# Moving the first half's expert choice and part of its scatters into the attention turns

## The reference

```python
x = x + tanh(g_xattn[0]) * attention(layernorm(x), ctx, ctx, mask, Wq, bq, Wk, bk, Wv, bv, Wo, bo)   # 16 heads of 8
x = x + tanh(g_ffn[0]) * ffn(layernorm(x))

# ffn: 2 shared experts for every token, and 2 of 8 routed experts by token
sh = gelu(xf @ sW1[s] + sb1[s]);  shared = mean_s(sh @ sW2[s] + sb2[s])       # hidden size 512
gates = xf @ rW + rb
topk_vals, topk_idx = top_k(gates, 2);  p = softmax(topk_vals)
y_e = gelu(xf @ W1[e] + b1[e]) @ W2[e] + b2[e]                                 # for the chosen e alone
return shared + sum over the two chosen e of p_e * y_e
```

## Time and profile before

| | |
|---|---|
| runs shown, median | 484.74 us |
| profiled execution, its span | 524.9 us |
| turns 5 to 17 of the attention (79.9 to 224.1) | 144.2 us |
| first gelu of the shared experts | at 249.2 us |
| shared experts, 16 units | 249.2 to about 361.6 us |
| routed experts, 39 tiles | 362 to 500 us |
| results gathered and added | 500 to 524.9 us |

### The profile page before, as it was taken

How to read it: one execution, slowest core, us unless ns; L and a number is a source line. 1 busy time by engine, 2 the same in 40 slices (tenths; PEclk the granted TensorE clock), 3 DMA queues, 4 the chain that set the end, 5 groups by cost and what they waited for, 6 DMA issues and landing times.

```text
span 524.9 us, 13531 instructions
## 1 busy us (share of the span) xinstructions
PE 415.9 (79%) x4611; PEld 297.2 (57%) x4611; DVE 397.8 (76%) x983; ACT 340.8 (65%) x674; POOL 315.9 (60%) x382
## 2 busy tenths in 40 slices
PE   0377979879998989776784989898999989998930
PEld 0245767758776877554341433344878777776720
DVE  7696769868778778987774896494888768886795
ACT  0536857657787877665663876495677567765743
POOL 9151524494987889598876376650466656666550
PEclk9998989899999999988997989999999999999985
DMA  8767863442333534540011011113122222244119
GB/s 226 223 197 202 223 146 80 103 101 75 78 87 84 114 82 142 178 164 17 26 51 45 27 41 41 47 36 81 36 78 77 70 72 86 67 132 138 58 44 280
DMA packets 71753, 53.19 MB, mean 101 GB/s; under 512 B 7473, under 2 KB 63548, under 8 KB 71688
## 3 DMA queue, kind: packets, MB, share of 16 engines
q1 hardware_dynamic: 64608, 42.96, 30.2%
q0 software_dynamic: 4544, 8.44, 4.6%
q10 hardware_dynamic: 2536, 0.94, 0.7%
HBM read 29.38 MB, written 24.33 MB: 102 GB/s over the span
## 4 chain that ended last, share of the span: by engine, by line
PE 25%; DVE 8%; issue 5%; another core or an unknown queue 5%; ACT 4%; POOL 2%; DMA 1%; ACTq 0%; DVEq 0%; POOLq 0%
PE pAtt L1123 9%; PE pE L1111 4%; PE pS L1111 4%; DVE HH L1490 3%; PE pAtt L1061 2%; PE pMix L1101 2%; PE pS L999 2%; ACT H L767 1%; POOL yd L622 1%; PE pE L999 1%; DVE HH L1486 1%; ACT G L803 1%; DMA YY<-yd 1%; DVE t_X L1543 1%
## 5 line engine op out<-in xcount | busy, mean ns | idle before, releaser
L622 POOL DMA_INDIRECT yd<-Y,XR x78 | 85.0, 1089 | 72.5 <-DVE Y L1529 45.4
L1234 DVE TENSOR_REDUCE t_MX<-pS 128x4 f32<-128x512 f32 x128 | 86.4, 682 | 24.0 <-PE pS L861 22.4
L720 ACT ACTIVATE PT<-pE,t_mbias,t_scl 128x512 f32<-128x512 f32 x128 | 97.1, 788 | 6.6 <-PE pE L861 6.4
L597 POOL DMA_INDIRECT xs<-t_STG,t_pos x64 | 64.2, 1002 | 36.5 <-issue 15.4
L1123 PE MATMUL pAtt<-t_W2h,HR 128*128 x624 | 65.3, 219 | 6.8 <-issue 5.5
L803 ACT ACTIVATE G<-pS,t_b1T,t_inv 128x256 f32<-128x256 f32 x78 | 40.0, 569 | 43.6 <-remote 39.3
L1490 DVE SCALAR_TENSOR_TENSOR HH<-H,t_sc,HH 128x512 f16<-128x512 f32 x64 | 48.4, 761 | 21.6 <-ACT HH L772 14.7
L1521 DVE SCALAR_TENSOR_TENSOR HR<-G,t_sc,HR 128x512 f16<-128x512 f32 x78 | 58.6, 751 | 2.8
L1123 PE MATMUL pAtt<-t_W2l,HR 128*128 x312 | 56.4, 219 | 3.4 <-issue 3.4
L1123 PEld LDWEIGHTS pAtt<-t_W2h,HR 128*128 128x128 f16 x624 | 50.0, 97 | 12.6 <-issue 10.9
L861 PE MATMUL pE<-t_Q,t_K 128*128 128x128 f16 x512 | 51.6, 225 | 5.8 <-DMA t_Q<-MPT 4.8
(11 more groups left out here) (276 smaller groups left out, 1044.5 us busy)
## 6 DMA issues: line engine op xcount, KB each, us to landing
xs<-t_padrow SPq DMA_DIRECT2D x10, 516.0 KB, 5.3
XR<-xs SPq DMA_DIRECT2D x39, 129.0 KB
scr<-QKS SPq DMA_DIRECT2D x16, 256.0 KB, 2.2
t_Q<-scr SPq DMA_DIRECT2D x16, 256.0 KB
t_K<-scr SPq DMA_DIRECT2D x32, 128.0 KB
t_STG<-in_W SPq DMA_DIRECT2D x7, 512.0 KB, 6.4
YY<-yd SPq DMA_DIRECT2D x14, 256.0 KB, 5.8
t_X<-in_x SPq DMA_DIRECT2D x4, 512.0 KB, 6.5
```

Source lines behind the costliest of these rows:

```text
L597: g.indirect_dma_start(k.xs, bass.IndirectOffsetOnAxis(ap=pos[:, n:n + 1], axis=0), k.PAY[:, n, :], None).then_inc(h.di[q], 16)
L622: g.indirect_dma_start(k.yd, bass.IndirectOffsetOnAxis(ap=XR[u][:, q, D:ROW], axis=0), Y[u][:, q, :], None, bounds_check=2 * T - 1, oob_is ...
L720: act.activation(PT[:, m % NPT], pE[g % 2][:], ACT.Exp, bias=k.mbias[:, bt:bt + 1], scale=k.scl[:, bt:bt + 1]).then_inc(s.exp, 1)
L1234: v.tensor_reduce(out=MX[:, n % G // 4, m % 2, m // 2::2], in_=pS[n % 2][:], axis=AX_X, op=ALU.max).then_inc(s.max, 1)
```

## The change

- The weight pieces come two a turn, from turn 5 (one) over turns 6 to 14 (two each) to turn 15 (one), in another order. The scaling is tensor_tensor with the scale repeated over the row, and no longer tensor_scalar.
- Row pairs 0 to 7 are normalised, transposed and gated two turns earlier (POOL turns 6 to 13, PE turns 7 to 14). The inverse deviations of pairs 0 to 7 come in four chains of two pairs (turns 6, 8, 10, 12) and no longer in two of four (turns 8, 12).
- The pieces of `first_part` stand in turn 14 (3), turn 15 (7) and turn 16 (the rest), and no longer in turns 17 to 19. PE's counting stands in turn 15, in another bank; DVE copies the prefixes out of it and then lets PE go on (new semaphore l.seen).
- 18 of the first 32 scatters stand in turns 16 to 19 (2, 5, 5, 6), ahead of the row pairs of each turn. The other 14 come after the last two row pairs. Those of the second half wait for a later count of h.lo.
- The first weight scales are computed in step 1 of turn 5, not in step 5. Padding is one transfer a turn in turns 5 to 14.

```diff
-    SPLIT = LAG + 3
-    FIRST_W2 = 4
-    UBODIES = END - SPLIT - 1
+    SPLIT = LAG + 2
-    SPLITS = ((0, 8), (0, 9), (0, 0), (0, 4), (1, 0), (0, 1), (0, 5), (1, 1), (1, 2), (1, 3), (0, 2), (0, 6), (1, 4), (0, 3), (0, 7), (1, 5),
+    SPLITS = ((0, 8), (0, 0), (0, 4), (0, 9), (0, 1), (0, 5), (1, 0), (1, 1), (1, 2), (0, 2), (0, 6), (1, 3), (0, 3), (1, 4), (1, 5),
...
+    split_done = lambda which, e: SPLITS.index((which, e)) + 1
+    FIRST_W2 = split_done(1, 0) - 1
+    FIRST_ROWS = NP // 2 - 1
+    SCATTERED = {16: 2, 17: 5, 18: 5, 19: 6}
+    PACED = 4
+    SECOND_FROM = 22
...
-    pR, pC = ([in_part(t[:, q, :]) for t in (pS[0], pM)] for q in range(2))
+    pR, pC = ([in_part(pM[:, slot + q, :]) for slot in (2, 0)] for q in range(2))
...
-        at = lambda j: min(max(j, 0) * UNITS // UBODIES, UNITS)
+        at = lambda j: min(max(2 * j - 1, 0), UNITS)
...
-        if not 9 <= t < END:
-            return ()
-        return (t - 9,) if t <= 16 else (2 * t - 26, 2 * t - 25)
+        if FIRST_ROWS <= t < FIRST_ROWS + NP // 2:
+            return (t - FIRST_ROWS,)
+        return (2 * t - 26, 2 * t - 25) if NP < t < END else ()
...
-    RSTD = {8: (0, 4), 12: (4, 4), 16: (8, 4), 18: (12, 2), 20: (14, 2)}
+    RSTD = {6: (0, 2), 8: (2, 2), 10: (4, 2), 12: (6, 2), 16: (8, 4), 18: (12, 2), 20: (14, 2)}
...
-                for n in {15: range(0, 3), 16: range(3, 6), 17: range(6, NE)}.get(t, ()):
-                    padding(n)
+                if LAG + 2 <= t < LAG + 2 + NE:
+                    padding(t - LAG - 2)
...
-                g.tensor_scalar(stg, stg, k.sc[:, sc:sc + 1], None, ALU.mult).then_inc(s.wh, 1)
+                g.tensor_tensor(stg, stg, view(k.sc, sc, [0, HID]), ALU.mult).then_inc(s.wh, 1)
...
+                if t == NP - 1:
+                    first_index(0)
+                    g.wait_ge(k.s_empty, 16 * NE)
+                for _ in range(SCATTERED.get(t, 0)):
+                    next(scattered)
                 for p in normalised_in(t + 1):
                     payload(p)
...
+            scattered = scatter_part(0, sum(SCATTERED.values()) + PACED)
+            turns(body)
+            for p in LAST:
+                payload(p)
+            for _ in scattered:
+                pass
+            first_index(1)
+            for _ in scatter_part(1, -SECOND_FROM):
+                pass
...
-                    if t == END - 2 and g == 1:
+                    if t == NP - 1 and g == 5:
                         prefixes(0)
...
+                link(v.tensor_copy(G2[:], pR[0]))
+                settle(v, l.seen)
...
-                    if t == LAG + 2 and g == 5:
+                    if t == LAG + 2 and g == 1:
                         first_scales()
...
-                    if t == END - 3 and g < G - 1:
+                    if t == NP - 2 and g > 4 or t == NP - 1 and g != 4 or t >= NP:
                         next(first, None)
-                    if t == END - 2 and g > 1 or t == END - 1:
-                        next(first, None)
+                    if t >= NP:
                         next(first, None)
```

74 lines of the change are left out of this document (41 added, 33 removed).

## The result

The changed kernel took 503.91 us (median of 4 runs, 502.13 to 504.45) against 485.60 us of the kernel before beside it (4 runs, 484.67 to 486.93): ratio 1.0367, interval 1.0339 to 1.0396, so 3.7% slower. I had forecast 482.2 us and a range of 474 to 491.

The account below looks back on a forecast made before the run. It took PE and POOL as nearly full in the attention's middle and DVE as the bound at its end. Terms +1.5 + 0.5 + 0.5 + 2 + 5 - 6.2 - 2.0 - 3.8 = -2.5 us on 484.74 gave 482.2 us, range 474 to 491.

Parts of the forecast that it names:

- growth of more than 0.5 us a turn: Sign for the middle turns: the prediction is wrong if they grow by more than 0.5 us.
- POOL's pass: Turns 9 to 13: two weight pieces and a pair take 12.0 us against a turn of 11.6; +1.5 us.
- POOL becomes the bound: Rival, turns 7 to 14: scaling at 1.56 us makes the pass outlast the turn; 490.2 us, chance 0.24.
- the rival built on that rule: Rival: two-input scaling takes 3.1 us, so POOL's pass takes 15.7 us in eight turns; 516 us, chance 0.02.
- POOL's hold on DVE: Nine turns: POOL's tensor_tensor scaling holds up DVE instructions, lengthening PE's wait; +0.5 us, ends 0 and +4.
- Four chains instead of two: Turns 6 and 10: two added 2.8 us chains nearly all hidden in DVE's free time; +0.5 us, ends 0 and +3.
- Padding and the second scale: SP's queue, tight in turn 7: padding delays the weights' maxima coming back; +2 us, ends 0 and +5.
- The pieces two a turn: POOL's pass: each of 20 pieces priced only by its scaling, 1.56 us becoming 1.24.
- The choice in turns 14 to 16: DVE takes the choice's 33 instructions: +0.5, +2.5 and +2 by turn, together +5 us, ends +2 and +9.
- Out of turns 17 and 18: PE's 3.54 us wait falls to 0.5; its 2.62 us and a later 0.5 go; -6.2 us, ends -3 and -7.
- Scatters and last pairs: POOL starts the last pairs at once, ending PE's 1.99 us wait in the shared experts; -2.0 us, ends 0 and -3.
- Waits without a cause: Units 4 and 5: unexplained ACT waits, perhaps from dense scatters; half of PE's 7.5 us taken, -3.8 us.

Follow-up runs that it names:

- e12: Changed kernel with one iteration instead of three in the chains of deviations of turns 6, 8, 10 and 12; ratio 1.0647 to the kernel before, on a slower chip.
- e2: Changed kernel with the weight pieces' scaling back as tensor_scalar, nothing else; 499.04 us, ratio 1.0277 to the kernel before.
- e11: As e17, but with the weight pieces scaled by tensor_scalar; 487.77 us against 485.32 for the kernel before, ratio 1.0038.
- e3: Changed kernel with expert choice, counting and scatters back where the kernel before has them; 492.09 us, ratio 1.0176 to the kernel before.
- e6b: As e3, but with row pairs and chains of deviations in the turns of the kernel before; ratio 1.0070 to that kernel, on a slower chip.
- e13: Kernel before with padding one piece a turn from turn 5 and the first weight scale at step 1; ratio 1.0068 to the kernel before, on a slower chip.
- e16: As e6b, but with weight pieces from turn 6, padding and first scale as in the kernel before; 483.29 us against that kernel's 485.17, ratio 0.9973.
- e17: As e16, but with the two chains of deviations begun behind the shifted maxima; 482.32 us, ratio 0.9955 to the kernel before.
- e10: Kernel before with only its two chains of deviations begun behind the shifted maxima; 487.97 us against 485.32, ratio 1.0065.
- e14: Changed kernel with the first half's scatters behind the last two row pairs, none inside the turns; ratio 1.0667 to the kernel before, on a slower chip.
- e8: Changed kernel run again, unaltered, as a base on the same chip; 502.50 us, ratio 1.0365 to the kernel before.
- e5b: Same kernel as e14, run again; ratio 1.0665 to the kernel before, on a slower chip.
- e7b: Changed kernel with each turn's scatters behind that turn's row pairs instead of ahead; ratio 1.0664 to the kernel before, on a slower chip.

## Why the prediction was wrong

First by stretches, forecast against measured, where the boundaries are those of the first table. Up to turn 14: +4.5 and +16.1 us. Turns 14 to 17: +2.0 and +4.3. Turn 17 to the first gelu: -3.2 and +0.6. From there on: -5.8 and -0.1. Together -2.5 and +20.9. About half of the miss is ahead of turn 14, where I had written that growth of more than 0.5 us a turn would show the prediction wrong: turns 9 to 12 grew by 0.7 to 2.2 us each.

By its own steps, against the traces that come without the stalls:

- *POOL's pass*, +1.5: nothing. The scaling is 1.04 us, below the whole range of 1.16 to 1.56 that I had kept, and turn 13 took 10.83 us. POOL's waits in these turns were beside the path (e12), and the rival "POOL becomes the bound" fell. e2 and e11 show that it would have been one at 1.56, with turns of 12.3 us, and e2 that this would have been the smaller loss. The Trainium skill's rule on two-input work ("GPSIMD Engine Reference", section 4.1) compares GpSimd with VectorE; I had taken it for a ratio between two forms on GpSimd, and so read the rows of both forms speak against it, 1.56 us with one tensor input and 1.04 with two. (The sum of the rival built on that rule comes to 515 us, not 516.)
- *POOL's hold on DVE*, +0.5: at least 2.4 to 4.3 us, by e2 against the five traces of the changed program, turn 5 to 14. I had the row that shows the hold, and its upper end of +4, and chose near the lower.
- *Four chains instead of two*, +0.5: this is the step that failed most. "DVE has 13.4 us free in the five turns, which hides nearly all" compares a sum of busy time with a sum of free time. A chain in steps 0 to 2 stands ahead of the shifted maxima, PE waits for these in step 3, and no free time later in the turn brings that back. The rows' earlier turns with the two added chains cost about 5 us (e3 against e6b); that the instructions behind step 3 cost nothing is e12's.
- *Padding and the second scale*, +2: +0.5 at turn 17 (e13). DVE's waits for the weights' maxima to come back did not grow.
- *The pieces two a turn*, priced at 0.3 us each in POOL's pass and nowhere else: this was missing. Turn 14 begins at 186.5 us in the kernel before, 190.7 in e16 (+4.2), 194.8 in e6b (+4.0 more, with the first piece in turn 5, the scale at step 1 and the padding), 199.6 in e3, and 199.7 and 202.6 in the two traces of the changed kernel. In e16 the cost is in the turns around the chains (turns 6, 7, 11 and 12: 13.70, 15.97, 13.65 and 13.00 us against 12.62, 13.92, 12.50 and 12.69), not in turns 9 and 10, which have none (11.05 and 11.27 against 11.08 and 11.55). With the chains behind the maxima the same pieces cost 0.9 us in turns 5 to 14 (e17, 110.6, against e10, 109.7) where they cost 4.0 with the chains ahead, both times scaled by tensor_tensor. So most of this term, too, is paid through the chains. Scaled by tensor_scalar they cost 5.9 even with the chains behind (e11, 115.6), POOL being the bound.
- *The choice in turns 14 to 16*, +5: too low, though the stretch looks right. Its +4.3 and +3.3 in the two traces hold a gain of 2.5 and 3.5 us in turn 16. I had booked such a gain with the waits of turn 17, whose cause stands ahead of the maxima of turn 17 and so inside this stretch; about 1 us of it comes from the pieces' leaving (turn 16 of e3). Against e3, which has the choice later, the stretch grew by 6.1 and 5.1 us; turns 14 and 15 alone took 6.8 us more than in the kernel before, where I had +3. No wait of PE in turns 14 to 16 is for its counting or for the copy behind it, so that price of nothing held.
- *Out of turns 17 and 18*, -6.2: the waits of 3.54 and 2.62 us went, as said. The gain of 4.6 us from turn 17 to the first gelu does not come from the choice but from the pieces' leaving, since e3 has it with the choice in its old place. *Scatters and last pairs*, -2.0: I had priced the scatters as POOL's time, not as five instructions ahead of row pairs that PE wants. Inside the turns they take the whole gain back, 5 us (e14). PE's wait for the last pairs (2.52 us in the kernel before) is gone in the changed kernel's first trace, which then leads by 1.8 us at the 21st gelu; by the 25th the lead is 0.2 us. In between the clock fell, to 0.64 where the kernel before has 1.00 (first line the changed kernel, second the kernel before). e8 keeps 1.00 there, and its last stretch is 0.9 us shorter:

```profile
294.00:298.00 4.00, 3.55 (x10) 1.37 (x11) 3.93 (x8) 2.91 (x5) 1.76 (x3) 0.64 0.10 33
...
275.00:279.00 4.00, 3.59 (x23) 1.83 (x24) 3.93 (x8) 3.56 (x6) 3.09 (x4) 1.00 0.16 54
```

- *Waits without a cause*, -3.8: they were not in the runs that were timed. That the profiled execution was 40 us longer than the runs was in view, and I argued from its rows all the same.

The low clock is a cost of its own that I did not price. In turn 12 to 13 the changed kernel took 13.77 us with the clock at 0.75 in one trace and 11.79 us at 1.00 in the other (e8), with PE's wait ahead of it 3.20 and 2.81 us: 2 us, of which up to 0.4 is the longer wait. It does not follow from the wait's length alone: e12 had the wait of 2.81 us too, a clock of 0.75, and 13.60 us.

What stays open: how the 4.2 us of e16 and the further 4.0 of e6b divide between hold, clock and turn 5; and what makes the relatives of the changed kernel (e12, e14, e5b, e7b) about 6.5% slower on two of the chips, where it is 3.7% slower elsewhere.
